# Attention probabilities merged by VectorE before the product with the values

## The chip, the cores and the metric

The kernel runs on one core of a Trainium2 chip. The metric is the device time of one execution in microseconds (us). Engines: TensorE (PE), VectorE (DVE), ScalarE (ACT), GpSimd (POOL), and SyncE (SP), which here only issues DMAs.

## The reference

One layer of a vision transformer on 64 images of 196 tokens, width 256, 16 heads of 16. The part that the change touches is attention with relative positions:

```python
term1 = einsum('bhqd,bhkd->bhqk', Q, K)
term2 = einsum('bhqd,kd->bhqk', Q, r);  term4 = einsum('hd,kd->hk', v, r)
scores = (term1 + term3 + _rel_shift(term2 + term4)) / sqrt(dk)
attn = softmax(scores, axis=-1)
out = einsum('bhqk,bhkd->bqhd', attn, V).reshape(B, S, H * dv) @ Wo + bo
```

`_rel_shift` moves row q to the left by an amount that depends on q. So the entries of a row before and up to the query (key <= q) come from one row of the position terms, key q+1 gets zero, and keys behind it come from the next row. The kernel therefore has two sets of scores, "main" (key <= q) and "upper" (key > q+1), and key q+1 is dealt with apart.

## The kernel before

The program has stages: `project` (patches, layer norm, Q, K, V), `attend` (attention), `route`, and three passes of `feed_forward`. Only `attend` is changed. It runs from about 690 to 1950 us of the profiled execution.

`attend` walks over 64 images, 4 groups of 4 heads each (`QUADS`), and 2 halves of 98 tokens each (`c`). I call one (group, half) a slot: an image has 8, numbered 2q + c, and the stage has 512. Each engine has its own program, and works in every slot in the fixed order of its own `position`; semaphores tie them together. In a slot two passes are worked on:

- The first pass finds the largest score of each row. It runs `LAG` = 6 groups (12 slots) ahead. PE's `stage_s` makes the upper scores in `psD` (one PSUM bank, L916, L919) and the main ones in `psS` (two banks of two heads, L929 to L932). DVE copies the upper scores over the main ones where the mask `later` says so (COPY_PREDICATED, L848, one for each bank) and takes the row maxima (TENSOR_REDUCE, L854, one for each bank). `psS` and `psD` stand once: PE may write a bank of `psS` for the next slot when its reduce has finished (`s_max`), and DVE copies in a bank when its scores are there (`s_ok`).
- The second pass computes the scores again, transposed and with the maximum taken off (`stage_e`: `psF` upper, `psE` main). ACT takes the exponentials: `after` from `psF` (L800), then the two halves of `probs` from `psE` (L803). POOL clears the forbidden part of `after` (L749) and then of the diagonal block of `probs` (L753, `clear_masked`). PE multiplies both with the values into `psO` in `stage_v`, one slot later: four matmuls with `probs` (L969, 196 columns) and four with `after` (L973, 98 columns), all added up.

Work once or twice per image hangs in fixed slots (`TAIL`): slots 1 and 4 transpose the output (L1001) and normalise it (DVE L884 to L888, then POOL `attn` L781); slots 2 and 6 transpose `attn` (L1010); slots 3 and 7 multiply with Wo (L1016), and DVE adds to the residual (L894); slot 5 transposes the maxima (L993, DVE L876). DVE combines the maxima in slot 3 (L861 to L871). POOL besides has `values` (L737) and `bias` (L743) behind its `clear_masked` in slots 2 and 6, one of the two at a time, and `ev` (L773) in slot 5.

On PE the order in a slot is `stage_s`, `stage_e`, `stage_v` of the slot before, tail. On DVE it is copies, reduces, tail.

Of the kernel before, what the change touches and what calls it, by code (L numbers as in the profile page):

```python
# [506 lines left out]
def attend(nc, d):  # L507
# [8 lines left out]
    with stage(nc) as ctx:  # L516
# [56 lines left out]
        made = semaphore(nc, ctx, "p2_constants_made")  # L573
        s_ok, chosen, s_max = signal("s_in_psum", 6), signal("s_selected", 4), signal("row_max", 4)
        e_ok, p_ok, kept = signal("e_in_psum", 6), signal("probs", 6), signal("probs_masked", 4)
        corners = semaphore(nc, ctx, "p2_corner_rows")
# [30 lines left out]
        with nc.Block() as block:  # L607
            @block.sync
            def _(sp):
                for s in (*stacks, tokens_in, h0_in, m_in, h1_out, rinsed):  # L610
                    s.open(sp)
                for dst, name in ((ident, "ident"), (never32, "never")):
                    sp.dma_start(dst[:], d[name]).then_inc(masks_in, 16)
# [107 lines left out]
            def _(pool):  # L721
# [69 lines left out]
            def _(act):  # L791
# [32 lines left out]
            def _(dve):  # L824
                for s in (chosen, s_max, mch, mrow_ok, nrm, num_ok, h1_ok):
# [6 lines left out]
                dve.wait_ge(masks_in, 16 * 2)  # L832
                nc.vector.tensor_copy(ident16[:], ident[0:TILE, 0:TILE]).then_inc(made, 1)
                nc.vector.memset(outside[:], NEVER).then_inc(made, 1)
                nc.vector.tensor_scalar(later[:], never32[:, 0:TILE], 0.0, None, ALU.is_lt).then_inc(made, 1)  # L835
                dve.wait_ge(made, 3)

                def position(i, r, c):
                    s, k, n, q, g, u = where(i, r)
                    s1, k1, n1, q1, g1, u1 = where(i, r + LAG)  # L840
                    if known(s1, 0, SLOTS):
                        if q1 == 0 and c == 0:
                            dve.wait_ge(mch.sem, mch.at(k1 - 2))
# [12 lines left out]
                    if q1 == 3 and c == 1 and known(k1, 0, IMAGES):
# [42 lines left out]
            def _(pe):  # L899
                for s in (s_ok, e_ok, pv_ok, mtr, ott_ok, at_ok, wo_ok):  # L900
                    s.open(pe)
                pe.wait_ge(made, 3)
                pe.wait_ge(keys_in[0], 16 * 3)

                def stage_s(s, q, g, u, c, n):
# [56 lines left out]
                def stage_v(s, n, q, g, u, c):  # L962

                    pe.wait_ge(kept.sem, kept.at(s, 2 * c + 2))
                    if c == 0:
                        pe.wait_ge(v32_ok.sem, v32_ok.at(n))
                        pe.wait_ge(ot_ok.sem, ot_ok.at(s - 1))
                    for j in range(4):
                        nc.tensor.matmul(psO[32 * j:32 * j + 32, 0:S], v32[u][:, 2 * g + c, 4 * q + j, :],  # L969
                                         probs[c][:, j // 2, (j % 2) * S:(j % 2 + 1) * S],  # L970
                                         start=(c == 0), stop=False)
                    for j in range(4):
                        last = nc.tensor.matmul(psO[32 * j:32 * j + 32, c * TILE:(c + 1) * TILE], v32[u][:, 2 * g + c, 4 * q + j, :],  # L973
                                                after[c][:, j, :], start=False, stop=(c == 1))
                    last.then_inc(pv_ok.sem, 1)
# [1018 lines left out]
```

## Time and profile before

| | |
|---|---|
| median of 3 runs | 3627.04 us (3626.7 to 3637.05) |
| the profiled execution | 3636.08 us, its span 3634.4 us |
| mean granted TensorE clock | 0.939 |
| PE busy, whole span | 3229.9 us (89%) |
| DVE busy | 2623.7 us (72%) |
| ACT, POOL busy | 1498.6 us (41%), 1617.8 us (45%) |

The span is what the profile saw; the time is that of the whole execution. All durations further down come from this one execution. PE's busy time is from the start of a matmul to its modelled end, waiting included where one matmul overlaps the next, so 100% there doesn't mean that every cycle works. `x2` in a row of a timeline means two instructions put together, with the time from the first's start to the last's end.

### The profile page before, as it was taken

Reading aid. Unit: us, or ns where it says so; the run is one execution under the profiler, and the core shown is the slowest. Engines: PE = TensorE matmul, PEld = TensorE weight load, DVE = VectorE, ACT = ScalarE, POOL = GpSimd, SP = SyncE. Lnnn points to the kernel's source line nnn. Section 1 sums busy time; section 2 is a strip of 40 time slices with the busy share of each in tenths; the row PEclk is TensorE's granted clock in tenths of the full one; section 3 lists DMA queues with packets and bytes.
Section 4 is the critical chain, followed back from the end, with each engine's and each line's share of the span. In section 5 each row is a group of like instructions: output and inputs, shape, how many; then the busy total and the mean of one; then the engine's idle time right before and its main releaser. Section 6 shows DMA issues by size and latency. Waiting matters only on the chain. (4 is left out here: it accounts for less than half of the span.)

```text
span 3634.4 us, 89293 instructions
## 1 busy us (share of the span) xinstructions
PE 3229.9 (89%) x34825; PEld 2526.0 (70%) x34881; DVE 2623.7 (72%) x6129; ACT 1498.6 (41%) x2991; POOL 1617.8 (45%) x1965
## 2 busy tenths in 40 slices
PE   6999999399999999999996722999599999998997
PEld 6888887378888888888883311778377777775876
DVE  5888888568888888888884676554266666665887
ACT  3444444056666666666663310332133333332221
POOL 2555555256666666666662010577200000004776
PEclk9999999579999999999998855999799999998999
DMA  4666665736556565665654611354333333225776
GB/s 141 185 185 197 195 186 161 189 84 164 157 149 172 136 166 148 160 162 148 170 133 131 182 30 34 110 140 126 95 116 111 107 104 106 95 90 135 217 219 165
DMA packets 449244, 518.11 MB, mean 143 GB/s; under 512 B 64150, under 2 KB 418804, under 8 KB 448397
## 3 DMA queue, kind: packets, MB, share of 16 engines
q1 hardware_dynamic: 427376, 473.19, 46.1%
q0 software_dynamic: 21504, 39.94, 4.1%
q8 instruction: 245, 4.01, 0.5%
q14 instruction: 119, 0.97, 0.1%
HBM read 306.93 MB, written 215.94 MB: 144 GB/s over the span
## 5 line engine op out<-in xcount | busy, mean ns | idle before, releaser
L1281 POOL DMA_INDIRECT sb_ye<-scratch_ye,sb_table x224 | 240.8, 1075 | 805.6 <-DMA sb_gw<-scratch_gw 733.3
L854 DVE TENSOR_REDUCE p_mx<-p_psS 98x2 f32<-98x390 f32 (+1 forms) x1024 | 527.1, 556 | 0.0
L800 ACT ACTIVATE p_after<-p_psF 98x392 f32<-98x392 f32 x512 | 255.1, 498 | 480.6 <-PE p_psF L946 472.5
L803 ACT ACTIVATE p_probs<-p_psE 98x392 f32<-98x392 f32 x1024 | 450.1, 496 | 0.0
L848 DVE COPY_PREDICATED p_psS<-p_later,p_psD 98x196 f32<-98x196 uint32 x1024 | 330.6, 362 | 120.0 <-PE p_psS L932 111.4
L749 POOL TENSOR_SCALAR_AFFINE_SELECT p_after<-p_after 98x392 f32<-98x392 f32 x512 | 274.4, 536 | 243.2 <-ACT p_after L800 243.0
L1269 POOL DMA_INDIRECT scratch_xe<-sa_xs,sa_table x224 | 222.2, 992 | 205.6 <-DMA sa_xs<-scratch_xf 140.4
L753 POOL TENSOR_SCALAR_AFFINE_SELECT p_probs<-p_probs 98x392 f32<-98x392 f32 x512 | 274.5, 536 | 85.8 <-ACT p_probs L803 80.2
L969 PE MATMUL p_psO<-p_probs,p_v 98*32 98x196 f32 x4096 | 279.8, 345 | 2.0 <-POOL p_probs L753 1.7
L419 POOL TENSOR_TENSOR p_rt<-p_rt 128x784 f32<-128x784 f32 x64 | 187.1, 2924 | 122.7 <-DVE p_st L397 122.7
L103 PE MATMUL p_psH<-p_wh,p_xh 128*98 128x256 bf16 x768 | 211.5, 275 | 24.3 <-DVE p_xl L334 24.3
L916 PE MATMUL p_psD<-p_K,p_U 96*98 96x98 bf16 (+1 forms) x2048 | 187.8, 215 | 36.7 <-DVE p_later L835 29.0
L916 PEld LDWEIGHTS p_psD<-p_K,p_U 96*98 96x98 bf16 x2048 | 160.6, 128 | 73.4 <-DVE p_later L835 29.1
L103 PE MATMUL p_psH<-p_wl,p_xh 128*98 128x256 bf16 x768 | 211.3, 275 | 0.0
L103 PE MATMUL p_psH<-p_wh,p_xl 128*98 128x256 bf16 x768 | 211.2, 275 | 0.0
L946 PE MATMUL p_psF<-p_U,p_K 98*98 98x98 bf16 x2048 | 180.3, 211 | 28.8 <-DMA p_U<-p_mrow 28.8
L1387 DVE CAST ex_gh<-ex_g 128x512 bf16<-128x512 f32 (+1 forms) x256 | 106.3, 415 | 106.7 <-ACT ex_g L1322 87.4
L973 PE MATMUL p_psO<-p_after,p_v 98*32 98x98 f32 x4096 | 182.3, 250 | 0.0
L1389 DVE TENSOR_TENSOR ex_gl<-ex_g,ex_gh 128x512 bf16<-128x512 f32 (+1 forms) x256 | 171.4, 669 | 8.8
L1322 ACT ACTIVATE ex_g<-ex_psG,ex_b 128x512 f32<-128x512 f32 (+1 forms) x128 | 85.7, 669 | 219.7 <-PE ex_psG L103 219.7
L1322 ACT ACTIVATE ex_g<-ex_psG,ex_first_b 128x512 f32<-128x512 f32 (+1 forms) x128 | 85.7, 669 | 218.1 <-PE ex_psG L103 218.1
L946 PEld LDWEIGHTS p_psF<-p_U,p_K 98*98 98x98 bf16 x2048 | 147.5, 127 | 32.5 <-DMA p_U<-p_mrow 31.6
(300 smaller groups left out, 10110.7 us busy)
## 6 DMA issues: line engine op xcount, KB each, us to landing
scratch_stack<-p_st SPq DMA_DIRECT2D x64, 784.0 KB, 6.0
p_x<-in_x SPq DMA_DIRECT2D x32, 1176.0 KB, 9.5
p_L<-scratch_stack SPq DMA_DIRECT2D x192, 196.0 KB, 4.3
p_U<-scratch_stack SPq DMA_DIRECT2D x192, 196.0 KB, 4.4
scratch_xe<-p_zero SPq DMA_DIRECT2D x32, 1024.0 KB, 5.9
ex_xin<-scratch_xe SPq DMA_DIRECT2D x56, 512.0 KB, 4.0
scratch_ye<-ex_y SPq DMA_DIRECT2D x56, 512.0 KB
scratch_h<-p_h SPq DMA_DIRECT2D x32, 392.0 KB
```

The lines of the kernel that those rows point to most:

```text
L103: last = nc.tensor.matmul(out, a, b, start=start and k == 0, stop=stop and k == len(todo) - 1)
L749: nc.gpsimd.affine_select(after[c][:], after[c][:], pattern=[[0, 4], [-1, TILE]], compare_op=ALU.is_ge, fill=nothing, base=-2, channel_mul ...
L753: nc.gpsimd.affine_select(diagonal, diagonal, pattern=[[0, 4], [1, TILE]], compare_op=ALU.is_ge, fill=nothing, base=0, channel_multiplier= ...
L800: act.activation(after[c][:].rearrange("p h t -> p (h t)"), psF[:, 0:4 * TILE], ACT.Exp, scale=DK ** -0.5).then_inc(p_ok.sem, 1)
L803: act.activation(probs[c][:, b, :], psE[:, b, 0:PAIR], ACT.Exp, scale=DK ** -0.5).then_inc(p_ok.sem, 1)
L848: nc.vector.copy_predicated(own[:, :, c * TILE:(c + 1) * TILE], later[:].unsqueeze(1).broadcast_to([TILE, 2, TILE]), upper).then_inc(chose ...
L854: nc.vector.tensor_reduce(mx[g1][:, c, 4 * q1 + 2 * b:4 * q1 + 2 * b + 2], own, AX.X, ALU.max).then_inc(s_max.sem, 1)
L916: last = nc.tensor.matmul(psD[:, j * TILE:j * TILE + wide], U[u][0:STACK, h][:, mid], K[u][0:STACK, h][:, mid.start + 1:mid.start + 1 + wi ...
L946: last = nc.tensor.matmul(psF[:, j * TILE:(j + 1) * TILE], K[u][0:ROWS, h][:, mid], U[u][0:ROWS, h][:, mid], start=True, stop=True)
L969: nc.tensor.matmul(psO[32 * j:32 * j + 32, 0:S], v32[u][:, 2 * g + c, 4 * q + j, :], probs[c][:, j // 2, (j % 2) * S:(j % 2 + 1) * S], sta ...
L1269: nc.gpsimd.indirect_dma_start(out=d["xe"], out_offset=bass.IndirectOffsetOnAxis(ap=table[:, b * BLOCK + t, k:k + 1], axis=0), in_=xs[v][: ...
L1281: nc.gpsimd.indirect_dma_start(out=ye[v][u][:, t, k, :], out_offset=None, in_=d["ye"], in_offset=bass.IndirectOffsetOnAxis(ap=table[:, at ...
```

## The change

Three edits in `attend`.

1. The forbidden part of the main tile is no longer cleared by POOL. Instead DVE copies the (cleared) exponentials of `after` over it, with a new mask `past` (key > query in the diagonal block, made once at the start from a loaded table `maskE`). One tile `probs` then holds every probability.
2. `stage_v` multiplies only `probs`. The four matmuls with `after` are gone. PE waits for the new signal `merged` and not for POOL's; ACT waits for `merged` of two slots ago before it writes `after` again.
3. In the first pass DVE does its two copies as one instruction and its two reduces as one; PE's matmuls into `psS` wait once for the whole reduce, and DVE's copy waits once for all of them.

```diff
+        behind, past = sb("behind", [TILE, TILE], U32), sb("past", [TILE, TILE], U32)
 def clear_masked(s, c):   # POOL
     pool.wait_ge(p_ok.sem, p_ok.at(s, 3 * c + 1))
     nc.gpsimd.affine_select(after[c][:], ...).then_inc(kept.sem, 1)
-    pool.wait_ge(p_ok.sem, p_ok.at(s, 3 * c + 3))
-    nc.gpsimd.affine_select(diagonal, diagonal, ...).then_inc(kept.sem, 1)
 # ACT
     act.wait_ge(pv_ok.sem, pv_ok.at(s - 1, c + 1))
+    act.wait_ge(merged.sem, merged.at(s - 1, c + 1))
 # DVE
-    for b in range(2):
-        dve.wait_ge(s_ok.sem, s_ok.at(s1, 3 * c + b + 2))
-        nc.vector.copy_predicated(own[:, :, c * TILE:(c + 1) * TILE], later..., upper).then_inc(chosen.sem, 1)
-    for b in range(2):
-        dve.wait_ge(chosen.sem, chosen.at(s1, 2 * c + b + 1))
-        nc.vector.tensor_reduce(mx[g1][:, c, 4 * q1 + 2 * b:4 * q1 + 2 * b + 2], own, AX.X, ALU.max).then_inc(s_max.sem, 1)
+    own = psS[:, :, 0:PAIR].rearrange("p b (h t) -> p b h t", h=2)
+    dve.wait_ge(s_ok.sem, s_ok.at(s1, 2 * c + 2))
+    nc.vector.copy_predicated(own[:, :, :, c * TILE:(c + 1) * TILE], later..., upper).then_inc(chosen.sem, 1)
+    dve.wait_ge(chosen.sem, chosen.at(s1, c + 1))
+    nc.vector.tensor_reduce(mx[g1][:, c, 4 * q1:4 * q1 + 4]..., own[:, :, :, 0:S - 1 + c], AX.X, ALU.max).then_inc(s_max.sem, 1)
+    if known(s, 0, SLOTS):
+        dve.wait_ge(kept.sem, kept.at(s, c + 1))
+        dve.wait_ge(p_ok.sem, p_ok.at(s, 3 * c + 3))
+        diagonal = probs[c][:].rearrange("p b (h t) -> p (b h) t", h=2)[:, :, c * TILE:(c + 1) * TILE]
+        nc.vector.copy_predicated(diagonal, past[:].unsqueeze(1).broadcast_to([TILE, 4, TILE]), after[c][:]).then_inc(merged.sem, 1)
 # PE, stage_s: one wait ahead of both banks, one signal behind them
+    pe.wait_ge(s_max.sem, s_max.at(s, 1) if c else s_max.at(s - 1))
     for b in range(2):
-        pe.wait_ge(s_max.sem, s_max.at(s, b + 1) if c else s_max.at(s - 1, b + 3))
...
-        last.then_inc(s_ok.sem, 1)
+    last.then_inc(s_ok.sem, 1)
 # PE, stage_v
-    pe.wait_ge(kept.sem, kept.at(s, 2 * c + 2))
+    pe.wait_ge(merged.sem, merged.at(s, c + 1))
     for j in range(4):
-        nc.tensor.matmul(psO[...], v32..., probs..., start=(c == 0), stop=False)
-    for j in range(4):
-        last = nc.tensor.matmul(psO[...], v32..., after[c][:, j, :], start=False, stop=(c == 1))
+        last = nc.tensor.matmul(psO[...], v32..., probs..., start=(c == 0), stop=(c == 1))
```

DVE's order, before, in the middle of the stage: slots 4 to 6 of an image (`p_den` begins the normalising of slot 4, `p_mrow` is slot 5's).

```order
L848 COPY_PREDICATED p_psS<-p_later,p_psD 98x2x98 x2
L854 TENSOR_REDUCE p_mx<-p_psS 98x2 x2
L884 TENSOR_TENSOR p_den<-p_psM,p_en 98x16
L886 RECIPROCAL p_rden<-p_den 98x16
L888 TENSOR_TENSOR p_num<-p_psM,p_ev 98x256
L848 COPY_PREDICATED p_psS<-p_later,p_psD 98x2x98 x2
L854 TENSOR_REDUCE p_mx<-p_psS 98x2 x2
L876 COPY p_mrow<-p_psM 32x196
```

The same two slots of the changed program; L858 is the new merging copy.

```order
L848 COPY_PREDICATED p_psS<-p_later,p_psD 98x2x2x98
L852 TENSOR_REDUCE p_mx<-p_psS 98x4
L858 COPY_PREDICATED p_probs<-p_past,p_after 98x4x98
L888 TENSOR_TENSOR p_den<-p_psM,p_en 98x16
L890 RECIPROCAL p_rden<-p_den 98x16
L892 TENSOR_TENSOR p_num<-p_psM,p_ev 98x256
L848 COPY_PREDICATED p_psS<-p_later,p_psD 98x2x2x98
L852 TENSOR_REDUCE p_mx<-p_psS 98x4
L858 COPY_PREDICATED p_probs<-p_past,p_after 98x4x98
L880 COPY p_mrow<-p_psM 32x196
```

Every slot's first-pass pair is followed by a copy that belongs to the second pass, ahead of the tail and of the next first-pass copy.

POOL's order before, around slots 4 to 6 (`p_attn` is slot 4's, `p_ev` slot 5's, `p_h` is `bias` in slot 6):

```order
L753 AFFINE_SELECT p_probs<-p_probs 98x4x98
L781 TENSOR_TENSOR p_attn<-p_num,p_rden 98x256
L749 AFFINE_SELECT p_after<-p_after 98x392
L753 AFFINE_SELECT p_probs<-p_probs 98x4x98
L773 TENSOR_TENSOR p_ev<-p_vnext,p_en 98x512
L749 AFFINE_SELECT p_after<-p_after 98x392
L753 AFFINE_SELECT p_probs<-p_probs 98x4x98
L743 TENSOR_TENSOR p_h<-p_h,p_bo 98x512
```

And in the changed program:

```order
L751 AFFINE_SELECT p_after<-p_after 98x392
L779 TENSOR_TENSOR p_attn<-p_num,p_rden 98x256
L751 AFFINE_SELECT p_after<-p_after 98x392
L771 TENSOR_TENSOR p_ev<-p_vnext,p_en 98x512
L751 AFFINE_SELECT p_after<-p_after 98x392
L745 TENSOR_TENSOR p_h<-p_h,p_bo 98x512
```

`p_ev`, `p_h` and the copy of the values now stand right behind the select whose result DVE's merging copy waits for.

## Rows read from the trace of the kernel before

**Rows 1.** Busy time by engine in two stretches of the attention stage; PEclk is the granted clock.
```profile
740.00:772.60 32.60, 32.60 (x340) 25.73 (x339) 18.07 (x51) 13.25 (x33) 12.40 (x22) 0.50 0.11 34
860.00:1925.00 1065.00, 1050.16 (x17823) 862.94 (x17817) 893.88 (x2600) 662.78 (x1766) 704.04 (x1195) 1.00 0.59 154
```
**Rows 2.** Groups of instructions, 900 to 1900 us: count, busy us, mean ns, idle before.
```profile
L854 DVE TENSOR_REDUCE p_mx<-p_psS 98x2 f32<-98x390 f32 (+1 forms) x854 | 439.6, 556 | 0.0
L848 DVE COPY_PREDICATED p_psS<-p_later,p_psD 98x196 f32<-98x196 uint32 x854 | 274.4, 361 | 76.4 <-PE p_psS L932 75.3
```
**Rows 3.** Timeline of DVE: start, us, instruction, idle before.
```profile
1301.87 0.62 DVE L848 COPY_PREDICATED p_psS<-p_later,p_psD 98x196 f32<-98x196 uint32 x2
1302.40 1.03 DVE L854 TENSOR_REDUCE p_mx<-p_psS 98x2 f32<-98x392 f32 x2
1303.35 0.24 DVE L876 COPY p_mrow<-p_psM 32x196 bf16<-32x196 bf16 x1
...
1312.35 0.17 DVE L884 TENSOR_TENSOR p_den<-p_psM,p_en 98x16 f32<-98x16 f32 x1 [0.35 <-PE p_psM L1001]
...
1313.01 0.62 DVE L848 COPY_PREDICATED p_psS<-p_later,p_psD 98x196 f32<-98x196 uint32 x2
...
1316.47 0.33 DVE L861 TENSOR_TENSOR p_mf<-p_mx,p_cnext 98x32 f32<-98x32 f32 x1
1316.83 0.45 DVE L864 TENSOR_SCALAR p_nm<-p_mf 98x32 bf16<-98x32 f32 x1
...
1317.87 0.42 DVE L894 TENSOR_TENSOR p_h<-p_psM,p_h 98x256 f32<-98x256 f32 x1
```
**Rows 4.** Timeline of PE, one slot with the product with Wo.
```profile
1305.40 0.52 PE L932 MATMUL p_psS<-p_K,p_L 96*98 96x196 bf16 x4
...
1306.40 0.54 PE L969 MATMUL p_psO<-p_probs,p_v 98*32 98x196 f32 x8
1306.75 0.35 PE L973 MATMUL p_psO<-p_after,p_v 98*32 98x98 f32 x8
1307.03 1.11 PE L1016 MATMUL p_psM<-p_wo,p_attnT 128*98 128x256 f32 x4
```
**Rows 5.** Timeline: one slot's first scores, its exponentials, POOL's first select.
```profile
1199.93 0.21 PE L929 MATMUL p_psS<-p_K,p_L 96*98 96x98 bf16 x1
...
1200.74 0.50 ACT L800 ACTIVATE p_after<-p_psF 98x392 f32<-98x392 f32 x1 [1.04 <-PE p_psF L946]
...
1201.13 0.88 ACT L803 ACTIVATE p_probs<-p_psE 98x392 f32<-98x392 f32 x2
...
1201.34 0.54 POOL L749 TENSOR_SCALAR_AFFINE_SELECT p_after<-p_after 98x392 f32<-98x392 f32 x1
```
**Rows 6.** Timeline of ACT and POOL: the extra work of slots 4 to 6.
```profile
1302.04 0.62 POOL L781 TENSOR_TENSOR p_attn<-p_num,p_rden 98x256 f32<-98x256 f32 x1 [0.49 <-DVE p_num L888]
...
1303.15 0.24 ACT L814 ACTIVATE p_en<-p_ea 98x32 f32<-98x32 f32 x1
...
1303.85 1.06 POOL L773 TENSOR_TENSOR p_ev<-p_vnext,p_en 98x512 f32<-98x512 f32 x1
...
1305.99 1.28 POOL L743 TENSOR_TENSOR p_h<-p_h,p_bo 98x512 f32<-98x512 f32 x1
```
**Rows 7.** Timeline of DVE and of POOL near the stage's start.
```profile
706.62 0.51 DVE L864 TENSOR_SCALAR p_nm<-p_mf 98x32 bf16<-98x32 f32 x1
707.16 1.20 DVE L866 SCALAR_TENSOR_TENSOR p_nm<-p_mf,p_nm 98x32 bf16<-98x32 f32 x1
...
706.48 0.61 POOL L737 COPY p_v<-p_vraw 98x512 f32<-98x512 f32 x1
707.05 1.26 POOL L743 TENSOR_TENSOR p_h<-p_h,p_bo 98x512 f32<-98x512 f32 x1
```
**Rows 8.** Groups of instructions, 740 to 772.6 us, at the lower clock.
```profile
L854 DVE TENSOR_REDUCE p_mx<-p_psS 98x2 f32<-98x392 f32 (+1 forms) x18 | 9.3, 556 | 0.0
...
L864 DVE TENSOR_SCALAR p_nm<-p_mf 98x32 bf16<-98x32 f32 x2 | 0.4, 180 | 0.1
```

More of the change, by code:

```diff
@@ L573, in attend @@
         made = semaphore(nc, ctx, "p2_constants_made")
-        s_ok, chosen, s_max = signal("s_in_psum", 6), signal("s_selected", 4), signal("row_max", 4)
-        e_ok, p_ok, kept = signal("e_in_psum", 6), signal("probs", 6), signal("probs_masked", 4)
+        s_ok, chosen, s_max = signal("s_in_psum", 4), signal("s_selected", 2), signal("row_max", 2)
+        e_ok, p_ok, kept = signal("e_in_psum", 6), signal("probs", 6), signal("after_masked", 2)
+        merged = signal("probs_merged", 2)
         corners = semaphore(nc, ctx, "p2_corner_rows")
@@ L611, in _ @@
                     s.open(sp)
-                for dst, name in ((ident, "ident"), (never32, "never")):
+                for dst, name in ((ident, "ident"), (never32, "never"), (behind, "maskE")):
                     sp.dma_start(dst[:], d[name]).then_inc(masks_in, 16)
@@ L750, in clear_masked @@
                                             fill=nothing, base=-2, channel_multiplier=1).then_inc(kept.sem, 1)
-                    pool.wait_ge(p_ok.sem, p_ok.at(s, 3 * c + 3))
-                    diagonal = probs[c][:].rearrange("p b (h t) -> p (b h) t", h=2)[:, :, c * TILE:(c + 1) * TILE]
-                    nc.gpsimd.affine_select(diagonal, diagonal, pattern=[[0, 4], [1, TILE]], compare_op=ALU.is_ge,
-                                            fill=nothing, base=0, channel_multiplier=-1).then_inc(kept.sem, 1)
                 def position(i, r, c):
@@ L824, in _ @@
             def _(dve):
-                for s in (chosen, s_max, mch, mrow_ok, nrm, num_ok, h1_ok):
+                for s in (chosen, s_max, merged, mch, mrow_ok, nrm, num_ok, h1_ok):
                     s.open(dve)
@@ L831, in _ @@
                         nc.vector.memset(dst[STACK:CORNER, :, column:PAIR:S], value).then_inc(corners, 1)
-                dve.wait_ge(masks_in, 16 * 2)
+                dve.wait_ge(masks_in, 16 * 3)
                 nc.vector.tensor_copy(ident16[:], ident[0:TILE, 0:TILE]).then_inc(made, 1)
                 nc.vector.memset(outside[:], NEVER).then_inc(made, 1)
+                nc.vector.tensor_copy(past[:, 1:TILE], behind[:, 0:TILE - 1]).then_inc(made, 1)
+                nc.vector.tensor_scalar(past[:, 0:1], ident[0:TILE, 0:1], 0.0, None, ALU.is_equal).then_inc(made, 1)
                 nc.vector.tensor_scalar(later[:], never32[:, 0:TILE], 0.0, None, ALU.is_lt).then_inc(made, 1)
-                dve.wait_ge(made, 3)
+                dve.wait_ge(made, 5)
                 def position(i, r, c):
@@ new lines, in position @@
+                        upper = psD[:, 0:4 * TILE].rearrange("p (b h t) -> p b h t", b=2, h=2)
+                        dve.wait_ge(s_ok.sem, s_ok.at(s1, 2 * c + 2))
+                        nc.vector.copy_predicated(own[:, :, :, c * TILE:(c + 1) * TILE],
+                                                  later[:].unsqueeze(1).unsqueeze(1).broadcast_to([TILE, 2, 2, TILE]),
+                                                  upper).then_inc(chosen.sem, 1)
+                        dve.wait_ge(chosen.sem, chosen.at(s1, c + 1))
@@ new lines, in position @@
+                        nc.vector.tensor_reduce(mx[g1][:, c, 4 * q1:4 * q1 + 4].rearrange("p (b h) -> p b h", b=2),
+                                                own[:, :, :, 0:S - 1 + c], AX.X, ALU.max).then_inc(s_max.sem, 1)
+                    if known(s, 0, SLOTS):
+                        dve.wait_ge(kept.sem, kept.at(s, c + 1))
+                        dve.wait_ge(p_ok.sem, p_ok.at(s, 3 * c + 3))
+                        diagonal = probs[c][:].rearrange("p b (h t) -> p (b h) t", h=2)[:, :, c * TILE:(c + 1) * TILE]
+                        nc.vector.copy_predicated(diagonal, past[:].unsqueeze(1).broadcast_to([TILE, 4, TILE]),
+                                                  after[c][:]).then_inc(merged.sem, 1)
@@ L901, in _ @@
                     s.open(pe)
-                pe.wait_ge(made, 3)
+                pe.wait_ge(made, 5)
                 pe.wait_ge(keys_in[0], 16 * 3)
@@ L968, in stage_v @@
                     for j in range(4):
-                        nc.tensor.matmul(psO[32 * j:32 * j + 32, 0:S], v32[u][:, 2 * g + c, 4 * q + j, :],
-                                         probs[c][:, j // 2, (j % 2) * S:(j % 2 + 1) * S],
-                                         start=(c == 0), stop=False)
-                    for j in range(4):
-                        last = nc.tensor.matmul(psO[32 * j:32 * j + 32, c * TILE:(c + 1) * TILE], v32[u][:, 2 * g + c, 4 * q + j, :],
-                                                after[c][:, j, :], start=False, stop=(c == 1))
+                        last = nc.tensor.matmul(psO[32 * j:32 * j + 32, 0:S], v32[u][:, 2 * g + c, 4 * q + j, :],
+                                                probs[c][:, j // 2, (j % 2) * S:(j % 2 + 1) * S],
+                                                start=(c == 0), stop=(c == 1))
                     last.then_inc(pv_ok.sem, 1)
```

10 lines of the change are left out of this document (1 added, 9 removed).

## The prediction, made before the changed kernel ran

> **What bounds the kernel now.** I read busy time by stretch first. Only the attention stage is changed, so only its pace counts. Between 860 and 1925 us PE is busy for 1050 of 1065 us and DVE for 894, at a granted clock of 1.00 (the 2.4 GHz level) [rows 1]. The groups of instructions give the pace: 854 reduces in 1000 us, 16 per image, so 53.4 images, or 18.73 us per image of 8 slots [rows 2]. Next the timelines, to see who is late. DVE's copies sat idle for 76 us in 1000, for want of PE's scores [rows 2]. PE goes through a slot without a hole: first scores at 1305.40, product with the values at 1306.40, its second half at 1306.75, next work at 1307.03 [rows 4]. PE is the bound, with DVE 3 us per image behind it. So the question is what is left on each once work moves from PE to DVE.
>
> **PE gets shorter.** The matmuls with `after` occupy PE from 1306.75 to 1307.03 [rows 4]: 0.28 us per slot, 2.24 per image. PE alone would then need 16.5 us per image.
>
> **DVE, part by part.** One copy of 196 elements takes 0.361 us and one reduce of 390 takes 0.556 [rows 2]: 1.0 ns per element and 0.16 fixed. The pairs take 0.62 and 1.03 with the second instruction started before the first has ended, and from the first copy's start to the last reduce's end it is 1.56 (1301.87 to 1303.43) [rows 3]. Merged, the copy is 0.36 + 0.20 = 0.56, the reduce 0.556 + 0.39 = 0.95. The reduce now waits for the whole copy; between an instruction and one that depends on it lie 0.03 us (706.62 + 0.51 to 707.16) [rows 7]. Sum 1.54: merging the pairs saves 0.02, since the fixed part of the second instruction was already hidden. Its bounds are 1.40 (no gap, and fixed parts half as long) and 1.65 (the pairs' 0.62 + 1.03 unchanged).
>
> The Trainium skill ("VectorE: DVE Perf Modes", the section on the TRN2 errata) gives an instruction that reads PSUM 120 cycles plus one per element at 0.96 GHz. By that estimate the merged pair would be 0.53 + 0.94 = 1.47, some 35 us less over the stage than by my sum. The rows agree in the slope, while their pairs of 0.62 and 1.03 show that part of the fixed cost was overlapped; I go by the rows.
>
> The merging copy (392 elements, all in SBUF) is not in the trace. The nearest row by size gives 0.16 + 0.39 = 0.55; the ends are 0.36 (a copy of half as many) and 0.95 (a reduce of twice as many). I take 0.56. A following instruction starts 0.08 before the end (1302.40 + 1.03 against 1303.35) [rows 3], so it costs 0.48 in DVE's row: 3.84 us per image.
>
> Tails per image [rows 3]: normalising 0.66 twice (1312.35 to 1313.01); `mrow` 0.24 - 0.08 = 0.16; residual 0.42 - 0.08 = 0.34 twice; combining the maxima 1316.47 to 1317.87 = 1.40, of which 0.27 goes as L864 takes 0.18 where POOL isn't beside it [rows 8], and by the same reason I take 0.14 off L861: 1.0. Together 3.16. DVE without any wait: 8 x (1.54 + 0.40) + 3.16 = 18.7 us, as long as the whole image takes now. PE's gain is gone already; every wait on DVE is now a loss.
>
> **The wait that merging adds.** Before, PE filled one bank of `psS` while DVE reduced the other. Now PE may start only at R, the end of the whole reduce, and DVE's copy needs all of it: signal 0.05, matmuls 0.52 [rows 4], signal 0.05, so R + 0.62. DVE puts the merging copy into that hole, free at R - 0.08 + 0.48 = R + 0.40. A slot without tail is 0.62 + 1.54 = 2.16. The merging copy needs the exponentials: first scores 1199.93, `probs` complete 1202.01 [rows 5], so 2.15 after the scores' start, which is R + 0.04 at a pace of 2.16: just in time. The next copy starts at the later of R + 0.62 and (merging copy's start + 0.48 + tail). From R to R, by the slot whose tail lies between:
>
> slot 7: 0.04 + 0.48 + 0.34 + 1.54 = 2.40; slot 0: 2.16; slot 1: 0.04 + 0.48 + 0.66 + 1.54 = 2.72; slot 2: 2.16; slot 3: 0.40 + 1.34 + 1.54 = 3.28; slot 4: 0.40 + 0.66 + 1.54 = 2.60; slots 5 and 6: 2.16 each. Sum 19.64, so +0.91 per image.
>
> **POOL in DVE's way.** L866, a DVE instruction on 32 elements with both inputs in SBUF, took 1.20 us: it began at 707.16, POOL's `bias` had begun at 707.05 and ended at 708.31, DVE's at 708.36. L864 took 0.51 beside `values` (706.48 to 707.09) [rows 7] and 0.18 alone [rows 8]. DVE waits until POOL's instruction is through. The first-pass copies (one input in PSUM) show no such thing, 0.361 on average [rows 2]. The merging copy has mask and source in SBUF, and waits for POOL's select, behind which POOL at once starts its other work:
>
> The Trainium skill ("SBUF — State Buffer", the section on who interferes with whom) has it as a rule: a DVE instruction with two SBUF inputs shuts out, and is shut out by, a GpSimd instruction that reads SBUF, for its whole length. The trace agrees with 1.20 against 0.18; for a predicated copy no row shows it.
>
> - Slot 5: `ev` starts when ACT has `en`: 2.08 after the scores, 0.24 for `en` [rows 6], and signals, R - 0.15; it lasts 1.06 [rows 6] to R + 0.91. The merging copy would start at R - 0.08: a race lost by 0.07. Next copy at 0.91 + 0.48 + 0.16 = R + 1.55, not 0.62: +0.93.
> - Slot 2: `attn` waits for the normalising of slot 1, now behind the merging copy, and pushes the select. After slot 1's R: 0.52 merging copy, 0.74 normalising to its end, 0.09 signal, 0.62 `attn` [rows 6], 0.49 more for the select, 2.46 in all, 0.26 before slot 2's R. Then 1.28 of `bias` [rows 6] until R + 1.0, or 0.61 of `values` [rows 7] until R + 0.35. Next copy at R + 1.48 or 0.83: +0.86 or +0.21, mean +0.54.
> - Slot 6: the select ends about 1.1 before R, `bias` at R + 0.18: +0.02. But if slot 5's race is won, slot 6 is a us shorter and loses about 0.3 to 0.9 in its turn.
>
> Sum 19.64 + 1.49 = 21.1 us per image, +2.4. PE's V product waits for the merging copy, but a slot later, behind 1.0 us of other work; its order has 16.5 of 21.1 to do.
>
> **Lower clock.** Until 772.6 us the clock stood at 0.50 (1.2 GHz) with PE busy throughout [rows 1]; 18 reduces in 32.6 us [rows 8] are 29.0 us per image. Some 2 images ran so. There PE stays the bound: 8 x 0.56 less, 24.5: -9 us in all.
>
> **Sum.** 62 x 2.4 - 9 = +140 us. One more small load at the stage's start and three tiny mask instructions lie beside the loads of the stacks: nothing. 3636.08 + 140 = 3776 of the profiled execution, which is 9 over the median of 3627; waits I have overlooked can only add here, DVE being without slack, so I stay at 3775.
>
> **Rivals.**
> 1. The merging copy isn't shut out by POOL (or wins the races): 62 x 0.91 - 9 = +47, 3675 to 3685. For it: a predicated copy with one input in PSUM isn't. Against: L866.
> 2. Not slower: the ring hole closes, and DVE runs without a wait at 18.7 us per image. 0 x 62 - 9: 3618 to 3627. It needs the scores to be back by R + 0.40, and not 0.62, in all slots without tail; PE's 0.52 of matmuls alone forbids it, unless the merged pair is near its low end of 1.40. PE as the bound, at 16.5 (3480), would need the merging copy for a quarter of its price.
> 3. The clock never rises. Before, it rose only after 30 us of a PE without gaps; if PE with DVE's holes isn't given 2.4 GHz, an image takes 24.5: 64 x 24.5 = 1568 against 62 x 18.73 + 58 = 1219, +349: 3975. For it: the late rise. Against: at 1.2 GHz PE has 24.5 us of work against DVE's 21, so it is as dense as before; once up, it stayed up.
>
> **How the numbers follow.** Forecast (shut out by POOL in slots 2 and 5 or 6) 0.57, 3720 to 3850 with the merging copy anywhere up to 0.8 us. Rival 1: 0.24, 3650 to 3720. Rival 2 and anything quicker: 0.10, half of it faster. Rival 3: 0.07. Rest, slower in other ways: 0.02. Range 3660 to 3850 leaves out some 0.2. A difference of 0.3% (11 us) is about what can be told from none. Faster 0.06, same 0.04, slower 0.90.
>
> **What would show it.** PE's busy time falls and its waits for DVE grow; slots of about 2.2 us where there is no tail; the copy L848 single at 0.56 and the reduce at 0.95; the merging copy at 0.56 in most slots, and at 1 us and more beside `ev` and `bias`. If its mean is 0.56 with no long ones, rival 1 holds. If DVE is idle for less than 1 us per image, rival 2. If the granted clock from 800 to 1900 us is 0.50, rival 3. I am wrong altogether if PE is still the engine that everybody waits for.

## The result, and the profile after

| | before | after |
|---|---|---|
| median | 3626.87 us (3625.97 to 3637.05, 4 runs) | 3875.48 us (3866.0 to 3883.01, 4 runs) |
| ratio | | 1.0681, 95% interval 1.066 to 1.0702 |
| span of the profiled execution | 3634.4 us | 3872.6 us |
| mean granted TensorE clock | 0.939 | 0.907 |

Slower, as forecast, but by 248 us and not by 148. The forecast of 3775 us and its range up to 3850 were both exceeded. The whole difference lies in the attention stage: from its first copy to its last product with Wo it took 1260.8 us before and 1499.7 us after, 238.9 more, against 238.2 of the span.

First the busy time by stretch in the changed kernel, with the columns of [rows 1]: stretch, its length, busy us of PE, PE's weight loads, DVE, ACT and POOL, then the granted clock, the busy share of the DMA engines and their GB/s.

```profile
740.00:762.00 22.00, 22.00 (x212) 16.72 (x211) 16.67 (x30) 10.04 (x25) 5.72 (x10) 0.50 0.15 51
...
860.00:1925.00 1065.00, 935.46 (x11773) 697.06 (x11771) 971.27 (x1793) 556.65 (x1460) 389.69 (x612) 0.90 0.50 129
...
1298.40:1366.70 68.30, 58.23 (x817) 43.86 (x816) 65.40 (x123) 38.15 (x101) 26.47 (x43) 1.00 0.44 118
1366.70:1373.50 6.80, 6.80 (x55) 4.83 (x53) 5.64 (x8) 3.22 (x8) 2.69 (x4) 0.50 0.25 70
1373.50:1411.00 37.50, 31.78 (x447) 23.93 (x446) 35.51 (x69) 20.51 (x54) 13.67 (x23) 1.00 0.55 143
1411.00:1421.30 10.30, 10.30 (x87) 7.38 (x85) 7.85 (x11) 4.35 (x11) 3.41 (x5) 0.50 0.53 134
```

PE fell from 1050 to 935 us and DVE rose from 894 to 971: the bound has moved to DVE, as forecast. New is the clock column: 0.90 where it was 1.00. The last four rows show what a mean of 0.90 is made of. The clock isn't a little lower, it drops from 2.4 to 1.2 GHz for 3 to 10 us and comes back. Between 800 and 1900 us it did so in 33 stretches, 228.8 us together; in the kernel before, in none.

The groups of instructions from 900 to 1900 us, which answer to [rows 2]:

```profile
L852 DVE TENSOR_REDUCE p_mx<-p_psS 98x4 f32<-98x784 f32 x354 | 344.2, 972 | 12.2
L858 DVE COPY_PREDICATED p_probs<-p_past,p_after 98x392 f32<-98x392 uint32 x355 | 282.9, 797 | 15.4 <-ACT p_probs L802 9.5
...
L848 DVE COPY_PREDICATED p_psS<-p_later,p_psD 98x392 f32<-98x392 uint32 x355 | 200.0, 563 | 22.7 <-PE p_psS L934 13.7 <-PE p_psS L936 4.8
```

355 copies, 8 per image, are 22.5 us per image (18.73 before); 21.1 was forecast. The single copy (0.563) and reduce (0.972) have about the sizes of the forecast (0.56, 0.95). The merging copy, L858, has a mean of 797 ns. Its single ones are in DVE's timeline (start, length, instruction, idle before):

```profile
1356.45 0.56 DVE L848 COPY_PREDICATED p_psS<-p_later,p_psD 98x392 f32<-98x392 uint32 x1
1357.04 0.97 DVE L852 TENSOR_REDUCE p_mx<-p_psS 98x4 f32<-98x780 f32 x1
...
1360.28 0.60 DVE L858 COPY_PREDICATED p_probs<-p_past,p_after 98x392 f32<-98x392 uint32 x1
...
1366.19 1.36 DVE L858 COPY_PREDICATED p_probs<-p_past,p_after 98x392 f32<-98x392 uint32 x1
...
1369.08 1.15 DVE L858 COPY_PREDICATED p_probs<-p_past,p_after 98x392 f32<-98x392 uint32 x1
...
1373.92 0.42 DVE L898 TENSOR_TENSOR p_h<-p_psM,p_h 98x256 f32<-98x256 f32 x1 [1.12 <-PE p_psM L1017]
```

POOL in the same stretch, against which the long ones are read:

```profile
1366.03 1.06 POOL L771 TENSOR_TENSOR p_ev<-p_vnext,p_en 98x512 f32<-98x512 f32 x1
1368.00 0.54 POOL L751 TENSOR_SCALAR_AFFINE_SELECT p_after<-p_after 98x392 f32<-98x392 f32 x1 [0.91 <-ACT p_after L799]
1368.50 1.26 POOL L745 TENSOR_TENSOR p_h<-p_h,p_bo 98x512 f32<-98x512 f32 x1
```

The copy of 1.36 us began at 1366.19, `ev` had begun at 1366.03 and ended at 1367.09. The one of 1.15 began during `bias`. Alone it takes 0.60. Over the stage, slot 5 has a mean of 1.35, slot 2 of 1.15, slot 6 of 0.87, the other five 0.60 to 0.61.

The Trainium skill ("SBUF — State Buffer", the section on who interferes with whom) has it as a rule that a DVE instruction with two SBUF inputs waits out a GpSimd instruction that reads SBUF and began before it. A predicated copy with mask and source in SBUF follows it: 1.36 beside `ev` against 0.60, which is 0.76 more, of the 0.90 us that `ev` still had to run.

Last, PE's timeline: three products with the values at the higher clock, and some matmuls after the drop at 1366.70:

```profile
1359.08 0.54 PE L973 MATMUL p_psO<-p_probs,p_v 98*32 98x196 f32 x8
1359.55 1.11 PE L1017 MATMUL p_psM<-p_wo,p_attnT 128*98 128x256 f32 x4
...
1361.66 0.54 PE L973 MATMUL p_psO<-p_probs,p_v 98*32 98x196 f32 x8
1362.24 0.65 PE L1002 MATMUL p_psM<-p_ident,p_ot 128*98 128x128 f32 x4
...
1363.72 0.54 PE L936 MATMUL p_psS<-p_K,p_L 96*98 96x196 bf16 x4 [0.61 <-DVE p_mx L852]
...
1364.74 0.54 PE L973 MATMUL p_psO<-p_probs,p_v 98*32 98x196 f32 x8
1365.09 0.25 PE L994 MATMUL p_psM<-p_ident,p_nm 98*32 98x98 bf16 x2
...
1366.33 0.24 PE L933 MATMUL p_psS<-p_K,p_L 96*98 96x98 bf16 x1 [0.63 <-DVE p_mx L852]
...
1369.51 0.87 PE L936 MATMUL p_psS<-p_K,p_L 96*98 96x196 bf16 x4
```

PE has a hole of 0.6 us ahead of its scores at 1363.72 and at 1366.33, waiting for the single reduce; in [rows 4] it had none. Four matmuls into `psS` take 0.54 at 2.4 GHz and 0.87 at 1.2. The list of waits from 1000 to 2000 us (who waited <- for whom: us in all, times, the longest) has the sums:

```profile
PE p_psS L936 <- DVE p_mx L852: 60.5, 144, 0.6
...
PE p_psS L933 <- DVE p_mx L852: 28.1, 45, 0.6
...
PE p_psM L1011 <- POOL p_attn L779: 18.3, 44, 0.7
```

These are 89 us of waits for the reduce, in 189 of some 357 slots.

I then split the images of this trace by their clock, from 860 to 1925 us, each from its slot 4 to the next. The 24 that ran wholly at 2.4 GHz took 20.9 to 21.6 us, mean 21.1 (21.2 if the cut is made at other slots). The 23 with a drop took 23.4 to 25.3, mean 24.2. So at the full clock the forecast of 21.1 was met, and the surplus sits in the images with a drop. Of the 33 drops from 800 to 1900 us, 25 began in slots 5 and 6.

That gave the theories for the experiments. A: PE's holes make the clock fall, and the drops cost some 1.3 us per image; filling the holes with work on PE brings the time back. B: the surplus is DVE's own (longer copies, waits), the clock falls with it but costs nothing, since DVE is the bound.

### The profile page after: what moved, and what is told of

It is laid out like the page before. It is cut to its first block and busy times, and to the rows that moved or that the text cites. A ratio compares the mean times of both kernels' runs of the same rounds, so it can differ in the third digit from the quotient of the medians.

```text
span 3872.6 us, 80650 instructions
## 1 busy us (share of the span) xinstructions
PE 3311.6 (86%) x30785; PEld 2494.6 (64%) x30785; DVE 2925.9 (76%) x5619; ACT 1509.9 (39%) x2991; POOL 1358.3 (35%) x1453
## 5 line engine op out<-in xcount | busy, mean ns | idle before, releaser
L852 DVE TENSOR_REDUCE p_mx<-p_psS 98x4 f32<-98x780 f32 (+1 forms) x512 | 497.9, 972 | 17.6
L858 DVE COPY_PREDICATED p_probs<-p_past,p_after 98x392 f32<-98x392 uint32 x512 | 404.9, 791 | 48.2 <-ACT p_probs L802 36.3
L848 DVE COPY_PREDICATED p_psS<-p_later,p_psD 98x392 f32<-98x392 uint32 x512 | 288.6, 564 | 48.4 <-PE p_psS L934 27.2
L973 PE MATMUL p_psO<-p_probs,p_v 98*32 98x196 f32 x4096 | 303.3, 371 | 21.0 <-DVE p_probs L858 20.0
L103 PE MATMUL p_psH<-p_wh,p_xh 128*98 128x256 bf16 x768 | 211.7, 276 | 23.9 <-DVE p_xl L334 23.9
L920 PE MATMUL p_psD<-p_K,p_U 96*98 96x98 bf16 (+1 forms) x2048 | 198.8, 223 | 37.9 <-DVE p_later L836 29.3
L936 PE MATMUL p_psS<-p_K,p_L 96*98 96x196 bf16 x1024 | 150.9, 275 | 84.0 <-DVE p_mx L852 84.0
L950 PE MATMUL p_psF<-p_U,p_K 98*98 98x98 bf16 x2048 | 193.7, 221 | 10.1 <-DMA p_U<-p_mrow 10.1
L1017 PE MATMUL p_psM<-p_wo,p_attnT 128*98 128x256 f32 x512 | 181.5, 488 | 0.8 <-ACT p_attnT L818 0.8
L933 PE MATMUL p_psS<-p_K,p_L 96*98 96x98 bf16 x1024 | 144.3, 228 | 40.9 <-DVE p_mx L852 40.7
L950 PEld LDWEIGHTS p_psF<-p_U,p_K 98*98 98x98 bf16 x2048 | 163.2, 138 | 12.8 <-DMA p_U<-p_mrow 11.0
```

Of the source, the lines that this page charges most:

```text
L103: last = nc.tensor.matmul(out, a, b, start=start and k == 0, stop=stop and k == len(todo) - 1)
L848: nc.vector.copy_predicated(own[:, :, :, c * TILE:(c + 1) * TILE], later[:].unsqueeze(1).unsqueeze(1).broadcast_to([TILE, 2, 2, TILE]), up ...
L852: nc.vector.tensor_reduce(mx[g1][:, c, 4 * q1:4 * q1 + 4].rearrange("p (b h) -> p b h", b=2), own[:, :, :, 0:S - 1 + c], AX.X, ALU.max).th ...
L858: nc.vector.copy_predicated(diagonal, past[:].unsqueeze(1).broadcast_to([TILE, 4, TILE]), after[c][:]).then_inc(merged.sem, 1)
L920: last = nc.tensor.matmul(psD[:, j * TILE:j * TILE + wide], U[u][0:STACK, h][:, mid], K[u][0:STACK, h][:, mid.start + 1:mid.start + 1 + wi ...
L950: last = nc.tensor.matmul(psF[:, j * TILE:(j + 1) * TILE], K[u][0:ROWS, h][:, mid], U[u][0:ROWS, h][:, mid], start=True, stop=True)
```

## The experiments

The pace is 8000 us over the number of full-width first-pass copies or reduces (16000 over half-width ones) from 900 to 1900 us; the two counts differ by at most two at the edges, which is 0.1 us at most. The clock is that of the same stretch.

| kernel | median us | ratio to before (95%) | us per image | clock |
|---|---|---|---|---|
| before | 3627 | | 18.7 | 1.00 |
| after | 3875.5 | 1.0681 (1.066, 1.0702) | 22.5 | 0.90 |
| `pe_filler` | 3799.5 | 1.0476 (1.0458, 1.0493) | 21.3 | 1.00 |
| `pool_after_merge` | 3809.0 | 1.0487 (1.0444, 1.053) | 21.7 | 0.92 |
| `halves_kept` | 3804.5 | 1.0492 (1.0474, 1.0511) | 21.4 | 0.95 |
| `pairs_joined_only` | 3683.1 | 1.0152 (1.0135, 1.0169) | 19.5 | 1.00 |
| `pool_after_and_filler` | 3750.4 | 1.0345 (1.0328, 1.0362) | 20.5 | 1.00 |
| `pool_after_halves` | 3723.8 | 1.027 (1.0253, 1.0287) | 20.1 | 0.99 |
| `all_three_undone` | 3731.0 | 1.0292 (1.0276, 1.0309) | 20.2 | 1.00 |
| `half_product_left_out` | 3611.6 | 0.9948 (0.9931, 0.9965) | 18.6 | 0.99 |
| `merge_in_even_slots` | 3668.8 | 1.0118 (1.0101, 1.0135) | 19.5 | 0.98 |
| `before_with_filler` | 3728.3 | 1.0283 (1.0266, 1.0301) | 20.3 | 1.00 |
| `before_warmed` | 3631.2 | 1.0024 (1.0013, 1.0034) | 18.7 | 1.00 |

**`pe_filler`**, on the changed kernel: PE makes the upper scores three times over in 6 of 8 slots, with the same result.

```diff
-                    for j in range(4):
+                    for j in list(range(4)) * (1 if (2 * q + c) in (0, 4) else 3):
```

> The changed kernel, with PE making the upper first-pass scores three times over instead of once in six of the eight slots, ahead of its wait for the reduce, in the hole that it has there. 8 x 6 more matmuls per image give about 2.2 us more PE work. Theory (the 1.2 us per image beyond 21.2 come from stretches at 1.2 GHz, which the clock falls to after PE's holes): granted clock near 1.00 after the first images, an image 21.2 us, time 3790 to 3820 us. Rival (the clock's drops cost nothing much, since VectorE is the bound in them too, and the longer images have another cause): 3875 us or more, as PE's work only grows. Third: the clock doesn't rise for it; then 3900.

Its busy time by stretch, in the columns above:

```profile
860.00:1925.00 1065.00, 996.24 (x14898) 778.11 (x14897) 1021.09 (x1901) 580.87 (x1550) 414.55 (x650) 1.00 0.53 137
```

More work on PE made the kernel 76 us faster. The clock stands at 1.00 without one drop, the merging copy is as long as before (791 ns), and the pace of 21.3 is close to that of the undisturbed images, 21.1 to 21.2. Theory B would have had no gain, or a loss. A holds in what the drops cost, and in that this work in the holes prevents them; other work was not tried.

**`pool_after_merge`**, on the changed kernel: POOL starts `values`, `bias` and `ev` only when the merging copy is through.

```diff
+                    if (c == 0 and r % 2 == 1 and known(s, 0, SLOTS)) or (c == 1 and q == 2 and known(k, -1, IMAGES - 1)):
+                        pool.wait_ge(merged.sem, merged.at(s, c + 1))
```

> The changed kernel, with POOL waiting for the merging copy of its slot before it starts its other work there (values, bias, ev), so that none of them can shut the copy out. Theory (shut-out costs 0.5 us in slot 2 and 0.9 to 1.4 us in slots 5 and 6 together): the merging copies all take 0.61 us, an image takes about 1.4 us less, 62 x 1.4 = 85 us, and as PE then has shorter holes some of the clock's drops go too: 3740 to 3790 us. Rival (the long copies lie beside another wait anyway): copies of 0.61, but time within 10 us of 3875.

Its merging copy in the groups of instructions from 900 to 1900 us, as all such rows below:

```profile
L860 DVE COPY_PREDICATED p_probs<-p_past,p_after 98x392 f32<-98x392 uint32 x370 | 222.7, 602 | 25.3 <-ACT p_probs L804 11.3 <-POOL p_after L751 6.8
```

The long copies are gone, 602 ns on average. Images at the full clock took 20.4 us on average (most of them 20.3), so POOL's shut-out costs 0.8 net of what POOL's wait costs elsewhere; 1.4 was expected, and the time of 3809 missed the expected 3740 to 3790. Drops remain (177.2 us in 18 stretches from 800 to 1900). Its four times differ by more than others do (3794 to 3830), and the trace is that of the slowest.

**`halves_kept`**: the changed kernel with copies and reduces in pairs as before (edit 3 undone, with its signals). **`pairs_joined_only`**: edit 3 alone, on the kernel before.

```diff
+                        for b in range(2):
+                            dve.wait_ge(s_ok.sem, s_ok.at(s1, 3 * c + b + 2))
...
-                        dve.wait_ge(s_ok.sem, s_ok.at(s1, 2 * c + 2))
```

> Edits 1 and 2 alone: the first pass's copies and reduces stay in two halves, one for each PSUM bank. Theory (merging the pairs exposes PE's filling of psS, 0.62 us, of which the merging copy hides 0.40): slots without tail go from 2.2 to 1.98, about 0.9 us per image less, 55 us: 3800 to 3830 us, and less if the clock drops go as well. Rival (one instruction instead of two is worth its fixed part of 0.1 to 0.15 us each): 3900 to 3950 us.

> Edit 3 alone, on the kernel before. Theory: each slot takes the longer of PE's work (1.86 us without tail, 2.3 to 2.8 with) and the ring of reduce, filling and copy (2.16; about 3.2 in slot 3), so 20.1 us per image in place of 18.7, +85 us: 3700 to 3720 us. Rival (slots lend each other slack, as VectorE's sum is 18.3 us with the ring in it): within 20 us of 3627. Third (fewer instructions are a gain): below 3620.

`halves_kept` came out at 3804, within its range, but not by the expected 0.9 us per image alone. Its undisturbed images took 20.6 to 20.7, 0.5 less than those of the changed kernel, and the time at the lower clock went from 228.8 to 112.6 us (800 to 1900). `pairs_joined_only` took 3683, between its theory (3700 to 3720) and its rival.

The groups of `pairs_joined_only`:

```profile
L851 DVE TENSOR_REDUCE p_mx<-p_psS 98x4 f32<-98x784 f32 (+1 forms) x409 | 397.7, 972 | 14.0
L847 DVE COPY_PREDICATED p_psS<-p_later,p_psD 98x392 f32<-98x392 uint32 x410 | 232.9, 568 | 129.5 <-PE p_psS L929 97.2 <-PE p_psS L927 25.8
```

Edit 3 alone costs 56 us on the kernel before, and 71 on top of the other two: it is a loss in either place. On the kernel before it is a new wait: DVE's copy sat idle for 129.5 us in 1000, against 76.4 [rows 2]. Beside the other edits its price shows in the clock as well (0.95 with pairs, 0.90 without). With the clock up and POOL's wait in both it is 19 us (`pool_after_and_filler` 3750, `all_three_undone` 3731, below).

On the changed kernel again: **`pool_after_and_filler`** has POOL's wait and the filler, **`pool_after_halves`** POOL's wait and the pairs, **`all_three_undone`** all three.

> The changed kernel with both: POOL waits for the merging copy, and PE repeats the upper scores in its holes. Theory (three separate costs: VectorE's row and the ring +0.9 us per image, shut-out +1.5, clock +1.2): only the first is left, granted clock 1.00, an image 19.6 to 19.9 us, time 3680 to 3700 us. Rival (the two costs are one, the clock falls because of the shut-out): no better than the better of the two alone, 3800. Rival 2 (the filler stretches PE's slots once VectorE is quicker): 3730 to 3780.

> Edits 1 and 2 with the first pass in halves, and POOL waiting for the merging copy. Theory: the ring and the shut-out are gone, VectorE's row of 18.7 to 19.0 us per image is left; but PE has 16.5 us of work in it and no filler, so the clock falls at times: 3650 to 3720 us. Rival (no drops, as PE is then denser than in the changed kernel): 3630 to 3645 us.

> Edits 1 and 2, first pass in halves, POOL after the merging copy, and the filler: no ring, no shut-out, no clock drops. Theory (what is left is VectorE's own row, 8 x (1.56 + 0.53) + 3.2 = 19.9 us per image with the merging copy at 0.61): 3690 to 3710 us. Rival (the filler costs more here than the few drops that pool_after_halves still has): 3730 us or more.

Reduce and merging copy in the groups of `pool_after_and_filler`:

```profile
L854 DVE TENSOR_REDUCE p_mx<-p_psS 98x4 f32<-98x784 f32 (+1 forms) x391 | 380.2, 972 | 13.5
L860 DVE COPY_PREDICATED p_probs<-p_past,p_after 98x392 f32<-98x392 uint32 x390 | 234.9, 602 | 27.1 <-POOL p_after L751 11.6 <-ACT p_probs L804 6.4 <-issue 0.3
```

The merging copy in those of `pool_after_halves`:

```profile
L863 DVE COPY_PREDICATED p_probs<-p_past,p_after 98x392 f32<-98x392 uint32 x398 | 240.0, 603 | 39.8 <-POOL p_after L751 21.3 <-ACT p_probs L804 9.7
```

All three missed their ranges on the slow side. With drops and shut-out both gone the changed kernel still takes 3750 and not 3680 to 3700. The number is that of the rival, by which the filler stretches PE's slots, but its mechanism has little part in it: an image takes 20.5 with the filler and 20.4 at the full clock without, and DVE's first-pass copies were idle for 10.3 us in 1000. The rest is what DVE's longer row, its waits and the single buffer of `psS` cost.

With the pairs back it is 3724, and there the filler is of no more use (3731, as its rival had it): hardly a drop was left for it to prevent (23.9 us at 1.2 GHz from 800 to 1900). 97 us above the kernel before remain, nearly all of them from edits 1 and 2 with POOL's wait. At the full clock an image takes 20.0 there. DVE is busy for 947 us in 1000 (845 before), and its merging copy sat idle for 39.8 more, 0.8 us per image, for POOL's select and ACT's exponentials.

**`before_with_filler`** puts the same filler into the kernel before.

> The kernel before with the same filler as pe_filler. It shows what the filler costs where PE has no holes. Theory (PE was the bound, 48 more matmuls per image of 0.045 us each): 2.2 us more per image at 2.4 GHz, more at 1.2 GHz: 3750 to 3780 us. Rival (PE had hidden slack in the kernel before, and the filler is free anywhere, so pe_filler says nothing of holes): within 15 us of 3627.

Its first-pass copies:

```profile
L848 DVE COPY_PREDICATED p_psS<-p_later,p_psD 98x196 f32<-98x196 uint32 x788 | 249.5, 362 | 146.2 <-PE p_psS L932 119.0 <-PE p_psS L930 27.2
```

103 us slower, where 123 to 153 were expected: the same matmuls cost 1.6 us per image where PE has no holes. So the filler is no gift in itself, and its gain in the changed kernel is the clock's.

**`half_product_left_out`** is the kernel before without its four matmuls of `after` with the values.

```diff
-                    for j in range(4):
-                        last = nc.tensor.matmul(psO[...], v32..., after[c][:, j, :], start=False, stop=(c == 1))
```

> The kernel before without the four matmuls with the upper exponentials in each slot: this leaves out that part of the product with the values, nothing else changes. It shows what edit 2 is worth by itself. Theory (PE is the bound before, 0.28 us per slot): an image goes from 18.7 towards 17.0, with VectorE at 15.8 close behind: 3510 to 3560 us if the clock holds. Rival (the matmuls lie in the shadow of other PE work, the next operation waits for the first four anyway): 3600 to 3627 us. Third: the clock falls for want of PE work: above 3600 with a granted clock under 0.97.

Its reduces and copies:

```profile
L854 DVE TENSOR_REDUCE p_mx<-p_psS 98x2 f32<-98x390 f32 (+1 forms) x860 | 443.1, 557 | 0.0
L848 DVE COPY_PREDICATED p_psS<-p_later,p_psD 98x196 f32<-98x196 uint32 x858 | 280.7, 361 | 70.0 <-PE p_psS L932 58.1
```

The matmuls that edit 2 removes are worth 14 us here, and not the 67 to 117 of the theory. Part of their gain is lost to the clock, which was low for 13.7 us from 800 to 1900: images without a drop took 18.35 us against 18.75, some 25 us over the stage. DVE's copies still sat idle for 70.0 us in 1000 (76.4 before). The rival has the number. Its mechanism (the next operation waits for the first four matmuls anyway) is true in part, as the section after this one shows.

**`merge_in_even_slots`** merges in slots with c = 0 only (POOL waiting for it, pairs kept) and lets POOL clear the diagonal in the others; the second product is gone in the merged slots alone.

```diff
-                    pe.wait_ge(kept.sem, kept.at(s, 2 * c + 2))
+                    pe.wait_ge(kept.sem, kept.at(s)) if c else pe.wait_ge(merged.sem, merged.at(s))
```

> A mixed form: first pass in halves; VectorE merges, and PE leaves out the upper product, only in the even slots (0, 2, 4, 6); in the odd ones POOL clears and PE multiplies both as before; POOL waits for the merging copy before values and bias. Theory (VectorE 15.8 + 4 x 0.5 = 17.8 us per image, PE 18.7 - 4 x 0.28 = 17.6): 3575 to 3610 us, quicker than both. Rival (PE gains less than 0.28 per slot): 3620 to 3640. Third: coupling of the two engines near balance costs what is gained: 3640 or more.

Its merging copy:

```profile
L869 DVE COPY_PREDICATED p_probs<-p_past,p_after 98x392 f32<-98x392 uint32 x206 | 125.3, 608 | 37.9 <-ACT p_probs L810 37.9
```

42 us slower, where 17 to 52 less were expected: the third case holds. It is somewhat under half of the 97 for all slots, but not because the price goes with the number of merging copies. Images without a drop took 19.1 us, 0.35 more than before, against 1.25 more in `pool_after_halves`; much of the rest goes with the four drops of 10.2 us each from 800 to 1900.

**`before_warmed`**: 24 matmuls of the identity on PE ahead of the first second-pass product, while PE waits for the maxima.

```diff
+                    if s == 0 and c == 0:
+                        for _ in range(24):
+                            nc.tensor.matmul(psO[:, 0:128], ident[:], ident[:], start=True, stop=True)
```

> The kernel before with 24 matmuls of the identity (128 x 128 x 128, fp32, into psO, which nobody reads yet) ahead of the second pass's first slot, where PE waits some 14 us for the maxima to come back by DMA. Theory (the clock rises on PE work that fills the array, and then holds through the attention stage): the rise comes at about 735 and not 772 us; the 1.4 images that were done in that time at 29 us then take 18.7 each, so 10 to 15 us less: 3612 to 3618 us. Rival (the clock rises only by the attention work itself, or falls again in the first slots): within 5 us of 3626.

Its busy time by stretch:

```profile
719.80:726.60 6.80, 3.07 (x28) 2.88 (x26) 0.00 (x0) 0.00 (x0) 0.00 (x0) 1.00 0.80 253
726.60:771.00 44.40, 41.41 (x429) 33.07 (x430) 21.51 (x59) 17.41 (x43) 15.63 (x28) 0.50 0.09 30
771.00:800.00 29.00, 28.13 (x481) 23.18 (x479) 24.47 (x72) 17.52 (x47) 19.35 (x32) 1.00 0.67 168
```

The clock rose at 719.8 us, then PE stood idle for 6.7 us before the next product, the clock fell at 726.6, and it rose for good at 771.0, hardly sooner than before (772.6). No gain: the rival holds, and the time is 7 us more (3631 against 3624 for the kernel before, measured beside it).

No version that computes everything beats the kernel before.

## Why the prediction was wrong, point by point

The direction and the new bound were right. So was the pace at the full clock, but by luck, since two errors of 0.7 to 0.8 us cancel in it. Per image, in us; 62 to 64 images make the 238.9 of the stage:

| term | forecast | measured | from |
|---|---|---|---|
| DVE's row and the ring | +0.91 | +1.7 | 20.4 at the full clock in `pool_after_merge`, less 18.73 |
| shut-out by POOL | +1.49 | +0.8 | 21.2 less 20.4 |
| TensorE's clock | 0 | +1.3 | 22.5 less 21.2 |
| sum | +2.4 | +3.8 | |

- **The step that failed** is on the clock. Rival 3 asked only whether it would ever rise, and was set aside with "once up, it stayed up". It did rise, at 762.5 us, and did not stay up. `pe_filler` shows it: without drops the time is 76 us less, 3799, within the range that I gave. I had looked at the two ends, never and always, and at PE's load at 1.2 GHz. The same text leaves PE without work for 4.6 us of an image at 2.4 GHz ("16.5 of 21.1 to do"), and that was not set against the clock that PE without holes had had. A further case between the two ends, drops for a fifth of the stage, was missing from the range. That DVE is the bound doesn't shelter the kernel: at 1.2 GHz the ring of R + 0.62 has matmuls of 0.87 in place of 0.54, and DVE waits 1.12 us for the product with Wo. In the waits from 900 to 1900 us:

```profile
DVE p_h L898 <- PE p_psM L1017: 27.5, 21, 1.4
```

  In `pe_filler` the same instruction never waited. From the copy of slot 7 to the next it takes 3.55 us on average in the changed kernel (4.6 where more than half of it ran at 1.2 GHz, 21 times) and 2.54 in `pe_filler`: 1.0 of the 1.2 between the two paces is lost there, the other 0.2 in slot 6 (2.48 and 2.25).
- **The first term** was 0.8 too small. Copy and reduce together take 1.56 (1356.45 to 1358.01) in place of 1.54, and the merging copy 0.60 in place of 0.56: at most 0.16 and 0.3 in 8 slots. Most of the rest is a wait that the sum had at almost nothing ("just in time"): the merging copy sat idle for 27.1 us in 1000 in `pool_after_and_filler`, some 0.5 per image, for POOL's select and for the exponentials. Slots 3 and 7 take 3.52 and 2.66 us there against 3.28 and 2.40. The split was wrong too. The sum had DVE's row at no loss (18.7) and the ring at 0.91; without the ring and the shut-out an image still took 20.0 (`pool_after_halves`, undisturbed ones), so the row with its waits costs 1.3 and the ring 0.4.
- **Shut-out.** The mechanism and slots 5 and 2 were right, the sum of 1.49 was 0.8. The copies are longer by 0.75, 0.55 and 0.27 in slots 5, 2 and 6, 1.6 together, but not all of it is lost. With the clock up in both, `pe_filler` against `pool_after_and_filler`, slot 5 takes 2.90 and 2.23 us, slot 2 2.55 and 2.21, slot 6 2.25 in both. That is 1.0 for the shut-out in place of 1.49; slots 3 and 7 give 0.25 of it back, being longer with POOL's wait (3.39 and 3.52, 2.54 and 2.66).
- **PE's shorter work.** I took 0.28 us per slot off PE. From the product's first matmul to the next work it takes 0.47 ahead of the product with Wo (1359.08 to 1359.55) against 0.63 in [rows 4], and 0.35 ahead of the bf16 transposition (1364.74 to 1365.09) against 0.52 before. That is 0.17 per slot, 1.3 to 1.4 per image. I had read that the second half began 0.35 after the first (1306.40 to 1306.75) as if the next work could begin there too; it begins 0.12 later in all slots but the one with the bf16 transposition. (The 0.58 from 1361.66 to 1362.24 is another thing: that transposition waited for DVE's residual L898. Where it doesn't wait, it is 0.47 as well.) So the gain of 2.24 per image was mis-sized. Nor is that all had in time: `half_product_left_out` gained 0.4 per image, and where the rest went no run separates. It did not matter here, since DVE's row ate it.
- **Merging the pairs saves nothing** was right (1.56 against 1.56), and that it makes a wait too, which costs 56 us alone. (The low end of 1.40 should have been 1.35 by its own terms, 0.48 + 0.87; nothing hangs on it.) The section of the Trainium skill on the TRN2 errata ("VectorE: DVE Perf Modes"), by which I had estimated 0.53 and 0.94, came near both instructions (0.563, 0.972). The rows, with 0.56 and 0.95, came nearer.
- **The first images.** Of the 9 us about 5 were had. The eight slots from 737 us on took 25.0 us (24.5 forecast) in place of 27.6, and the 25th first-pass copy began at 767.9 us in place of 773.1.
- **From the sum to the number.** The sum gives +140, which is 3767 on the median of 3627. I added it to the slower profiled execution and stayed at 3775.

What stays open is what exactly the clock answers to. Ahead of the drop at 1366.70 two slots in a row had holes of 0.6 us, but no run separates the length of the holes from what PE computes in all. PE's busy time by itself does not put the runs in order: in `merge_in_even_slots` it was busy for 969 us in 1000 and the clock was low for 41.0 us (800 to 1900), in `pe_filler` it was busy for 935 and the clock never fell.

## What to carry to other kernels

Work moved from TensorE to an engine that thereby becomes the bound can be paid twice: once there, and once more if the holes that it leaves on TensorE take it off 2.4 GHz. Ask of every change that adds waits to a full TensorE what each stage costs with the clock at 1.2 GHz for a part of the time, as a case of its own. Two instructions that overlap in a two-bank ring were not made cheaper here by joining them, and they lost the ring. And what the removal of matmuls is worth is not the time from their start to the next work's: here that was 0.28 us, and without them the next work began 0.17 sooner.

## What the runs showed of the hardware

- The clock fell with PE busy for 88% of the time by its records (935.46 of 1065), and with no wait of PE for DVE or POOL longer than 0.7 us from 1000 to 2000; the two drops shown lasted 6.8 and 10.3 us. Repeating matmuls that give the same result again took out all drops between 800 and 1900 us, and made the kernel 2% faster.
- A merging copy in SBUF takes 0.60 us alone and 1.35 beside `ev`: taking POOL's work out of its way is worth 49 us of the whole time (3799 to 3750 with the clock up in both).
